# One hand-written order per engine in place of a repeated step, in a fused attention and FFN layer on one core

## The reference

```python
def attn_block(x):                                   # called on layernorm(x)
    n = layer_norm(x, ln1_w, ln1_b)
    Q = elu(n @ q_w.T + q_b) + 1; K = elu(n @ k_w.T + k_b) + 1; V = n @ v_w.T + v_b   # Q, K: 64 wide
    x = x + (causal_linear_attention(Q, K, V)) @ o_w.T + o_b
    h = gelu(layer_norm(x, ln2_w, ln2_b) @ f1_w.T + f1_b)                              # 1024 wide
    return x + h @ f2_w.T + f2_b
def ffn_block(x):                                    # called on layernorm(x)
    h = layer_norm(gelu(x @ absmean(W_fc).T), ln_w, ln_b)                              # 1024 wide
    return h @ absmean(W_proj).T
# absmean(W): each weight becomes -1, 0 or 1 by a threshold from the mean of |W|
x = x + attn_block(layernorm(x)); x = x + ffn_block(layernorm(x))
```

## Time and profile before

| what | value |
|---|---|
| median of 3 runs | 457.57 us (457.09 to 457.77) |
| span of the profiled execution | 455.2 us |
| instructions on TensorE, VectorE, ScalarE, GpSimd (busy) | 2942, 1200, 580, 224 |
| busy time of them | 437.5, 367.7, 310.7, 238.6 us |
| granted clock of TensorE | 1.00 in all windows |

### The profile page before, as it was taken

One profiled execution on the slowest core, in us unless ns is written; L12 is line 12 of the kernel. 1 busy time (PEld: TensorE's weight loads), 2 busy tenths in 40 slices (PEclk: granted clock), 3 DMA queues, 4 the chain that ended last, 5 costly groups with the idle time before them and its releaser, 6 DMA issues.

```text
span 455.2 us, 8867 instructions
## 1 busy us (share of the span) xinstructions
PE 437.5 (96%) x2942; PEld 395.5 (87%) x2942; DVE 367.7 (81%) x1200; ACT 310.7 (68%) x580; POOL 238.6 (52%) x224
## 2 busy tenths in 40 slices
PE   3898999999989999999999999999999999999997
PEld 3786897889978899889998999889988899888986
DVE  6899989877968878888788879888799837867596
ACT  4887937895188855878668855779468854786173
POOL 3887215843358517682549525694496225181334
PEclk9999999999999999999999999999999999999999
DMA  7234010120111201030101201021100000000001
GB/s 241 118 99 181 0 49 1 48 71 1 9 62 48 69 3 48 34 102 6 48 25 48 69 2 46 25 70 48 48 24 1 24 1 1 25 1 24 0 25 48
DMA packets 13518, 20.41 MB, mean 45 GB/s; under 512 B 2720, under 2 KB 11040, under 8 KB 12960
## 3 DMA queue, kind: packets, MB, share of 16 engines
q1 hardware_dynamic: 13472, 19.84, 13.3%
HBM read 15.62 MB, written 4.22 MB: 44 GB/s over the span
## 4 chain that ended last, share of the span: by engine, by line
PE 76%; DVE 7%; issue 7%; POOL 4%; DMA 3%; ACT 1%; SPq 1%; POOLq 0%; DVEq 0%
PE bank_f L490 11%; PE bank_p L538 10%; PE bank_f L263 6%; PE bank_f L265 6%; PE bank_f L264 6%; PE bank_y L263 6%; PE bank_y L264 6%; PE bank_y L265 6%; PE bank_y L504 5%; PE bank_a L263 4%; PE bank_a L265 4%; PE bank_a L264 4%; DMA h<-in_f 2%; PE bank_a L271 1%; PE bank_f L271 1%
## 5 line engine op out<-in xcount | busy, mean ns | idle before, releaser
L1334 POOL TENSOR_TENSOR rs<-ve,neg_half 128x2 f32<-128x2 f32 x48 | 33.6, 702 | 134.1 <-DVE ve L972 131.2
L763 ACT ACTIVATE bank_f<-bank_f,f_bias 128x512 f32<-128x512 f32 x64 | 42.3, 660 | 37.8 <-PE bank_f L265 36.9
L263 PE MATMUL bank_y<-wf_hi,h_hi 128*128 128x256 f32 x240 | 67.2, 280 | 0.0
L264 PE MATMUL bank_y<-wf_lo,h_hi 128*128 128x256 f32 x240 | 67.1, 280 | 0.0
L265 PE MATMUL bank_y<-wf_hi,h_lo 128*128 128x256 f32 x240 | 67.1, 279 | 0.0
L1035 DVE TENSOR_TENSOR h_lo<-bank_f,h_hi 128x512 fp32r<-128x512 f32 x60 | 41.3, 688 | 29.9 <-ACT h_hi L771 29.5
L1170 DVE SCALAR_TENSOR_TENSOR g_lo<-bank_y,vec,g_hi 128x256 fp32r<-128x256 f32 x128 | 55.5, 478 | 10.7 <-ACT g_hi L800 10.2
L800 ACT ACTIVATE g_hi<-bank_y,vec 128x256 fp32r<-128x256 f32 x128 | 53.4, 479 | 12.0 <-PE bank_y L504 10.3
L538 PE MATMUL bank_p<-wpj_t,g_hi 128*128 128x256 f32 x240 | 60.0, 286 | 0.0
L538 PE MATMUL bank_p<-wpj_t,g_lo 128*128 128x256 f32 x240 | 58.6, 280 | 0.0
L263 PE MATMUL bank_f<-z2T_hi,wf_hi 128*128 128x512 f32 x128 | 52.4, 410 | 3.0 <-DVE h_lo L1035 1.9
(11 more groups left out here) (299 smaller groups left out, 1227.7 us busy)
## 6 DMA issues: line engine op xcount, KB each, us to landing
out<-y_yc SPq DMA_DIRECT2D x15, 256.0 KB, 2.2
u<-in_xt SPq DMA_DIRECT2D x6, 512.0 KB, 3.7
lines_b<-lines SPq DMA_DIRECT2D x6, 512.0 KB, 3.9
x_even<-in_x SPq DMA_DIRECT2D x8, 256.0 KB, 2.9
x_odd<-in_x SPq DMA_DIRECT2D x8, 256.0 KB, 3.1
h<-in_f SPq DMA_DIRECT2D x1, 1024.0 KB, 7.7
y_yc<-in_f SPq DMA_DIRECT2D x1, 1024.0 KB, 10.0
h<-in_fc SPq DMA_DIRECT2D x1, 1024.0 KB, 4.8
```

Of the source, the lines that this page charges most:

```text
L263: pe.matmul(ps, w[0], r[0], start=start, stop=False, skip_group_check=skip)
L264: pe.matmul(ps, w[0], r[1], start=False, stop=False, skip_group_check=skip)
L763: act.activation(bank_f[m % 2][:], bank_f[m % 2][:], ACT.Gelu, bias=f1_bias[:, m:m + 1]).then_inc(s["h_gelu"], 1)
L1334: pool.tensor_tensor(rs[n][:, 2 * h:2 * h + 2], ve[n][:, 2 * h:2 * h + 2], neg_half[:, 0:2], ALU.pow).then_inc(s[f"ln{n + 1}_rs"], 1)
```

## The change

`first`, `step` and `last` of TensorE, ScalarE, VectorE and GpSimd are each replaced by one function `order()` with every call of the whole program in a new order; SyncE's list is left as it was. The calls, their waits, their number and their instructions are the same. Both programs are written out call by call when they are built, so no loop exists on the chip in either. Of the lists the diff shows two lines for TensorE; the others change in the same manner.

```diff
@@ -541,65 +541,63 @@
-            def first():
-
-                qkb(); tu(0, 0); tu(0, 1); wvo_mm(); qk_mm(0); bvo(); fill(); scores(0); v_mm(0, 0); v_mm(0, 1)
-                attend(0, 0); attend(0, 1); attend(0, 2); tu(1, 0); attend(0, 3); tu(1, 1); f1b(); tz2(0, 0)
...
-            first()
-            for g in range(1, 4):
-                step(g)
-            last()
+            def order():
+                qkb(); wvo_mm(); tu(0, 0); tu(0, 1); bvo(); qk_mm(0); fill(); v_mm(0, 0); v_mm(0, 1); scores(0)
+                attend(0, 0); attend(0, 1); attend(0, 2); attend(0, 3); tu(1, 0); tu(1, 1); f1b(); tz2(0, 0)
...
+            order()
```

More of the change, by code:

```diff
@@ L825, in step @@
-            def step(g):
-                g_hi(g, 1, 0); gelu(g + 1, 0); h_hi(g + 1, 0); gelu(g + 1, 1); h_hi(g + 1, 1); u_hi(g + 2, 0)
-                g_hi(g, 1, 1); u_hi(g + 2, 1); gelu(g + 1, 2); h_hi(g + 1, 2); g_hi(g, 1, 2); g_hi(g, 1, 3)
-                gelu(g + 1, 3); h_hi(g + 1, 3); qk_exp(g + 2); gelu(g + 1, 4); h_hi(g + 1, 4); qk_hi(g + 2)
-                gelu(g + 1, 5); k_dup(g + 2); h_hi(g + 1, 5); gelu(g + 1, 6); h_hi(g + 1, 6); ae_hi(g + 2)
-                ad_hi(g + 2); gelu(g + 1, 7); h_hi(g + 1, 7); af_hi(g + 2); n1(g + 2); v_hi(g + 2, 0)
-                v_hi(g + 2, 1); z3_norm(g + 1, 0); z3_hi(g + 1, 0); z3_norm(g + 1, 1); z3_hi(g + 1, 1)
-                gelu3(g + 1, 0, 0); z2_norm(g + 2, 0); gelu3(g + 1, 0, 1); gelu3(g + 1, 1, 0); gelu3(g + 1, 1, 1)
-                g_hi(g + 1, 0, 0); z2_hi(g + 2, 0); gelu3(g + 1, 2, 0); g_hi(g + 1, 0, 1); gelu3(g + 1, 2, 1)
-                z2_norm(g + 2, 1); g_hi(g + 1, 0, 2); gelu3(g + 1, 3, 0); z2_hi(g + 2, 1); gelu3(g + 1, 3, 1)
-                g_hi(g + 1, 0, 3)
@@ L1409, in wf1_lo @@
                                    ALU.subtract).then_inc(s["wf1_lo"], 1)
-            def first():
-                consts(); ln1_rstd(0, 0); ln1_rstd(0, 1); n1_rstd(0); wf1_lo(0); ln1_rstd(1, 0); ln1_rstd(1, 1)
-                wf1_lo(1); wf1_lo(2); n1o(0); wf1_lo(3); wf2_lo(0); ln2_rstd(0, 0); wf2_lo(1); ln2_rstd(0, 1)
-                wf2_lo(2); n1_rstd(1); wf2_lo(3); xpb(0); xs(0); n1o(1); ln1_rstd(2, 0); ln1_rstd(2, 1)
-                ln3_rstd(0, 0); ln3_rstd(0, 1); x_mul(2, 0); x_add(2, 0); ln2_rstd(1, 0); x_mul(2, 1)
-                ln2_rstd(1, 1); x_add(2, 1); x_lo(2, 0); x_lo(2, 1); ln4_rstd(0, 0); n1_rstd(2); y_cpj(0)
-                correct(0, 0); xpb(1); xs(1); n1o(2); ln1_rstd(3, 0); ln1_rstd(3, 1); ln4_rstd(0, 1); correct(0, 1)
-                ln3_rstd(1, 0); ln2_rstd(2, 0); ln3_rstd(1, 1); ln2_rstd(2, 1); y_cpj(1); xpb(2); x_mul(3, 0)
```

375 lines of the change are left out of this document (217 added, 158 removed).

## The result

| | median us | runs |
|---|---|---|
| before, same chip | 457.67 | 457.09 to 459.0, 4 runs |
| changed | 460.69 | 460.28 to 461.2, 4 runs |

The ratio is 1.0067 with a 95% interval of 1.0048 to 1.0085: the new order is slower by 0.67%, 3.0 us. Forecast were 455.0 us, faster than before, with 451.5 and 459.3 as ends; the sign was wrong. The profiled execution has a span of 459.0 us, 3.8 more than that of before.

What follows compares the result with a forecast made beforehand. TensorE was taken to bound the kernel, busy 437.5 of 455.2 us. Holes were to change by −2.6 us up to 97 us and +0.1 after, −2.5 from 457.57: 455.0 us, range 451.5 to 459.3.

Steps and rivals of the forecast that it cites:

- The start: Up to `attend(0,0)`: `scores(0)` 1.13 us late at 20.7, `attend(0,0)` at 24.4 behind a 2.2 us hole, +0.4 us.
- Against it: the granted clock is 1.00 up to 24 us: Argument against a clock fall at the `attend(0,0)` hole: clock 1.00 up to 24 us despite 8.50 us idle.
- Rival (d): The new 2.2 us hole ahead of `attend(0,0)` lowers TensorE's clock to 1.2 GHz, costing some 3 us: 458.0; chance 0.04.
- `f1(0,0)` starts at 35.75: First FFN: `f1(0,0)` was to start at 35.75 us against some 35.96 before.
- I charge 0.6 for it at `attend(1,0)`: Batch 1 attention: `v_hi(1,0)` now stands behind `u_hi(2,0)`, which needs GpSimd's `x_add(2,0)`; charged 0.6 us.
- beside `f2`: First FFN: where `ternary(2)` and `(3)` were to run on VectorE; no separate cost given.
- the head: Everything up to 97 us: a sum of −2.6 us, with `fc(0,0,1)` at 73.0 against 75.36.
- Rival (c): The head's gain is given back, −2.6 becoming about −0.5: 457.2 us, no change that can be told; chance 0.13.
- From 97 us on: Rest of the program: −1.5 us for removed holes against +1.6 for new tight places, net +0.1 us.
- +1.6, with 1.0 and 4 as ends: Cost in us of new tight places behind 97 us, such as `f2(3,0)`, `tz3(2,1)`, `f1(3,0)`, `proj(2,1,0)` and `f1(6,3)`.
- rival (a): Queue backlog costs more in the steady steps, holes of 0.5 to 1.3 us in each of five: 459.1; chance 0.19.
- The sign: Profile mark for the costlier backlog: TensorE idle over 5 us from 130 to 350 us; forecast 1 to 3.

Runs made afterwards that it cites:

- e3: The changed kernel with nine more unread 512-wide matmuls on TensorE behind `scores(0)`, in the hole ahead of `attend(0,0)`: 459.48 us.
- e5: e3 with `u_hi(2,0)` on ScalarE moved behind `v_hi(1,1)`: 461.15 us over six runs on two levels.
- e6: e3 with `x_mul(2,0)`, `x_add(2,0)` and `x_mul(2,1)` on GpSimd behind `ln3_rstd(0,1)`, and ScalarE's `u_hi(2,0)` ahead of `u_hi(2,1)`: 460.2 us.
- e1: Order of the kernel before for calls begun by 97 us there, then the order of the changed kernel: 460.43 us.
- e4: The changed kernel with `scores(0)` ahead of `v_mm(0,0)` and `v_mm(0,1)` again, and `k_dup(0)`, `v_hi(0,0)`, `v_lo(0,0)` moved to fit: 461.48 us.
- e7: e3 with `ternary(0)` on VectorE behind `h_lo(0,1)` in place of ahead of `h_lo(0,0)`: 459.41 us.
- e8: e3 with `u_hi(5,1)` behind `gelu3(3,0,1)`, `ln4_stats(3,2)` behind `g_lo(3,0,1)`, `qk_exp(5)` behind `h_hi(4,1)` and `qk_sum(5)` behind `h_lo(4,1)`: 462.68 us.
- e9: The kernel before with `wf2_hi(3)` ahead of `abs_part(1)`, `selectors()` and `h_lo(0,1)` ahead of `ternary(0)`, and `ternary(1)` behind `h_lo(0,2)`: 457.19 us.
- e10: e9 with `proj(5,0,3)` on TensorE moved ahead of `f1(6,1)`: 457.78 us.
- e11: e3 with `u_hi(5,1)` on ScalarE behind `gelu3(3,0,1)` and `ln4_stats(3,2)` on VectorE behind `g_lo(3,0,1)`: 464.17 us.
- e12: e9 with `cpj()` behind `f1(0,6)`, `spread()` behind `f1(0,7)` and `rows()` on ScalarE behind `gelu(0,6)`: 458.54 us.
- e14: e3 with seven more unread matmuls behind `cpj()`, ahead of `attend(1,0)`, and `u_hi(5,1)` on ScalarE behind `gelu3(3,0,1)`: 460.2 us.
- e2: Order of the changed kernel up to the calls begun by 97 us there, then the order of the kernel before: 460.32 us.

## Why the prediction was wrong

**The start** was right: `scores(0)` at 20.95 (20.7 forecast), `attend(0,0)` at 24.71 (24.4), the hole 2.24 (2.2).

**"Against it: the granted clock is 1.00 up to 24 us"** is the first step that failed. Rival (d) had 0.04, and it came. Of the 8.50 us of idle time that I took as evidence 7.14 lay ahead of the first matmul of the program and 1.36 ahead of `scores(0)`, and a row at 1.00 there doesn't say what a hole of 2.2 us does behind work. Its size was about half of the 3 us that I gave it. Without it the changed kernel is still slower, as e3 shows.

**"`f1(0,0)` starts at 35.75"**: it came at 38.69. Of the 2.9 us the clock has 1.4, the late `attend(0,0)` 0.3, and 0.67 is a wait between `theta_sum(0)` and `tz2(0,1)` for VectorE's half of z (0.53 in its row, at 36.65); the rest, some 0.5, is not taken apart. From there the small steps were right: the hole ahead of `f1(0,2)` is 1.56, and `f1(0,3)` gains 1.57 on it (from 3.58 late to 2.01).

**"I charge 0.6 for it at `attend(1,0)`"** was 1.54, and its cause was another: e5 takes `u_hi(2,0)` away and the hole stays. I had worked out what `ternary(0)` costs beside GpSimd, and then let `ternary(2)` and `(3)` move "beside `f2`" without looking at what GpSimd does there. They cost 3.38 and 3.88 us in place of 2.03 and 2.04. The row and what I took from it were both in the prediction; they were applied to one of four. e6 confirms the cause: with nothing on GpSimd beside it `ternary(3)` takes 2.02 us and the hole is gone. So the head is +1.1 us and not −2.6. Rival (c), that the gain of the head is given back, had the direction, and more than that was given back.

**From 97 us on** the sum was +0.1, and the stretches give +2.75, the head of before with the new steps (e1) +3.1. The named places were mostly there: idle time from 97 to 130 us is 0.38 (1.17), the hole at 353.73 is gone, `f2(3,0)` waits 0.24 and `f1(6,3)` 0.31. What failed is "+1.6, with 1.0 and 4 as ends": the stretches from 131 to 285 are over by 3.93 against 0.40. The larger part of it is at places that I had not named, 0.39 at `fc(3,1,0)` in a cover that had held at three batches before, `tr(3,0,3)`, `f1(4,2)`, and many waits of 0.1 to 0.3. This is the mechanism of rival (a), but neither its price nor its sign as I wrote them. The price: its text puts 4.0 in the place of the 1.6, its sum adds 5.6; with 4.0 the sum would be 457.5 and not 459.1. Measured are 3.5. The sign was to be an idle time over 5 us from 130 to 350; it is 1.05, within the 1 to 3 of the forecast, because most of these waits hide in the busy time, and only the count from start to start shows them.

**The sum.** Between the forecast −2.5 and the measured +3.8 of the spans lie 6.3 us: 3.7 of them in the head (+1.1 for −2.6), 1.9 in the new tight places (3.5 for 1.6), 0.7 in the gains (−0.8 for −1.5). With the head as forecast the sum would have been about +0.1, no change that can be told; with the rest as forecast it would have been +1.2. So the head alone turned the sign, and the steps made most of the rest.

**The form of the argument** is behind both: I followed each new wait by itself and took every saved hole as gained time. The runs say otherwise. Of the kernels in which a named hole was removed by an order (e4, e6, e7, e8, e9, e10, e11, e12 and e14) none got faster; other waits took its place. In e4, e7, e9 and e12 it came back at another call that takes from VectorE's queue; in e6 one of the two new waits is for GpSimd, and in e8, e10, e11 and e14 a wait for ScalarE gave way to a longer one for VectorE. Only work put into a hole (e3) made the time shorter, and by way of the clock.

## What to carry to other kernels

In this kernel, with the bounding engine at 96% and the next one at 81%, most holes were the lateness of another engine's queue and not the fault of the call that waits; before crediting the removal of one, look for the next call that takes from that queue, and charge the lateness there. Judge a new order by the distances from start to start on the bounding engine and not by its idle time alone. Count the price of an operation anew at each place to which an order moves it, with what its neighbour engine does at that time. Leave no hole of 2 us behind work on TensorE if something, even unread matmuls, can stand in it. And read the mean clock of every run before comparing two medians: part of a difference, in e12 all of it, can be the clock of some of the runs.

## What the runs showed of the hardware

**The clock.** A hole of 2.24 us ahead of `attend(0,0)` brought the granted clock to 0.50 for some 3 us, which began 1.5 us behind the end of the hole, when TensorE was at work again; the four runs have the same mean clock, and with the hole filled it stayed at 1.00. Ahead of `attend(1,0)` the size of the hole does not tell what happens: behind 1.65 us in e2 and e11 and 1.69 in e4 the clock fell, behind 1.54 in the changed kernel, 1.57 in e5, 1.72 in e7 and 1.76 in e3 it didn't. Near that size one and the same order gives two times some 3.5 to 4 us apart, which a single run doesn't show.

**VectorE and GpSimd.** The two elementwise operations of a `ternary`, over 128 by 1024, took 2.02 to 2.04 us with GpSimd idle, and 3.4 to 4.3 us in the traces where 512-wide operations of GpSimd on two tensors ran beside most of both. One such addition (`n1o(1)` before, at 52.86) took 1.29 us. In the rows the operation that starts second pays: in e9 GpSimd's addition starts at 51.80, 0.22 us behind the second operation of `ternary(3)`, and takes 2.22 us, while the operation of VectorE keeps its 1.28; in the changed kernel the second operation of `ternary(2)` starts at 58.65 beside an addition that began at 58.02, and takes 2.20. No run was made for this order of starts alone.
